# Second cross attention: row sums from ScalarE into spare PSUM columns, another order of VectorE's step, one transpose for the ones matmuls

## The chip, the cores and the metric

The kernel runs on one core of a Trainium2 chip. The metric is the device time of one execution in microseconds (us). The engines are TensorE (PE, with its weight loads as PEld), VectorE (DVE), ScalarE (ACT), GpSimd (POOL) and SyncE (SP), which issues DMAs. Each has its own queue and they meet at semaphores.

## The reference

The input x has 32 blocks of 128 tokens with 128 features; each block has a context of 77 rows with 128 features. Four parts follow each other, each added to x: a cross attention with 16 heads of 64, a mixture of 8 experts (two per token), a second cross attention, and two layers of local attention with a gated feed-forward. The change is in the second cross attention:

```
x = x + L1_xattn(layernorm(x), ctx, ctx, mask)
q, k, v = layernorm(x) @ w_q.T, ctx @ w_k.T, ctx @ w_v.T     (16 heads of 8)
s = q k^T / sqrt(8), masked where mask == 0                  (128 x 77 per head)
out = softmax(s) @ v, heads joined, @ w_o.T
```

## The kernel before

The second cross attention is a software pipeline over the 32 blocks. In step i each engine runs its `body`, which works on several blocks at once: `it.b(n)` is block i - n. `c_tensor`, `c_scalar`, `c_vector` and `c_pool` hold the bodies. The pipeline is unrolled by hand; within a step the order of each engine's queue is the order of the code. Steps 0 to 3 interleave with the end of the experts, and steps 35 to 38 with steps 0 to 2 of the first layer (`c_into_d`). After steps 11, 15, 19 and 23 ScalarE and VectorE each split one layer weight into a high and a low part (L1290, L1296).

The stages of one block b, by lag:

- lag 0 and 1: GpSimd gathers the two expert answers of each token; VectorE adds them to X with their weights (L1446) and takes the row statistics (L1450 to L1455); GpSimd takes the root (L1043).
- lag 2: VectorE normalizes (L751), TensorE turns the block (L1379), VectorE evicts it (L1485).
- lag 3: TensorE projects queries, keys and values (L1351 to L1353) into PSUM slot 0; ScalarE evicts the high parts (L1407 to L1411); VectorE makes the low parts and the two key blocks, one for each part (L1459 to L1468). Semaphore `c_sp` counts these.
- lag 4: TensorE makes the scores in two halves of 8 heads, slot 2 and slot 3, two banks each: first a matmul that lays the mask (L1335), then three passes (L1340). In each bank 4 x 77 = 308 of 512 columns are used. VectorE takes the maxima of a half (`largest`, L1427), and ScalarE writes the 8 exponentials of that half to `c_p` (`exponentials`, L741).
- lag 5: TensorE turns the 8 probability blocks of a half (L1321) into slot 1, ScalarE evicts them to `c_pT` (L1397), once per half; the second half's transposes wait until the first half is evicted. Then TensorE multiplies by the values (L1367) and, with the same moving data, by blocks of ones (L1372): this gives the row sums, laid out as the output is. VectorE takes their reciprocal, 128x128 (L1480), and multiplies (L1482).
- lag 6: TensorE applies w_o (L1383), VectorE adds to X (L1487) and takes the statistics (L1491, L1036, L1038); GpSimd takes the root, which the first layer uses.

Orders of one step before. TensorE: transposes of half 0 (lag 5), scores of half 0 (lag 4), transposes of half 1, scores of half 1, projections, P times V and ones, transpose of the normalized block, w_o. ScalarE: `c_pT` of half 0, `c_pT` of half 1, exponentials of half 0, evictions of the projections, exponentials of half 1. VectorE: layernorm, maximum of half 0, maximum of half 1, expert answers and statistics, low parts and key blocks, reciprocal and product, eviction of the turned block, addition to X and statistics. The scores of a half wait for that half's exponentials of the step before (`ac_expa`, `ac_expb`), since they overwrite the same bank.

Of the kernel before, what the change touches and what calls it, by code (L numbers as in the profile page):

```python
# [12 lines left out]
ALU = mybir.AluOpType  # L13
# [3 lines left out]
NB = 32  # L17
# [95 lines left out]
def program(nc, out, x_in, ctx_in, mask_in, wq0_in, wkv0_in, wo0_in, nrm0_in, wg_in, w1e_in, w3e_in, w2e_in,  # L113
            l1_in, wqkv_in, qks_in, wol_in, lng_in, w1l_in, b1l_in, w2l_in,
            ident_in, band_in, rot_in, keyi_in, head_in):
    with ExitStack() as ctx:
# [34 lines left out]
        onesz = at("onesz", [128, 4, 4, DH1])  # L151
# [134 lines left out]
        c_["p"] = at("c_p", [128, 2, 16, SK])  # L286
        c_["rcT"] = at("c_rcT", [128, 128])
# [109 lines left out]
        def split_dve(e):  # L397
# [6 lines left out]
            e.memset(onesz[:], 0.0).then_inc(S("const"), 1)  # L404
# [10 lines left out]
            e.wait_ge(S("const"), 4)  # L415
            for j in range(4):
                e.memset(onesz[:, j, j, :], 1.0).then_inc(S("c_const"), 1)
# [56 lines left out]
        def a_tensor(e):  # L474

            e.wait_ge(S("split"), 2)
            e.wait_ge(S("const"), 4)
# [259 lines left out]
        def exponentials(e, t, slot, half, nbank, nk, done, scale=None, head=lambda h: h):  # L737
# [559 lines left out]

        def c_tensor(e):
            t = c_

            def body(it):
                if it.static and it.i == 2:
                    e.wait_ge(S("b_xl"), LAST + 1)
                    e.wait_ge(S("c_const"), 5)
# [5 lines left out]
                for half, slot in ((0, 2), (1, 3)):  # L1310
# [34 lines left out]
                if b is not None:  # L1345
# [3 lines left out]
                    e.wait_ge(S("ac_ch"), count(b, base=NB))  # L1349
                    c = t["c"][:, it.m(3, 4), :]  # L1350
# [11 lines left out]
                if b is not None:  # L1362
# [7 lines left out]
                    for j in range(4):  # L1370
# [16 lines left out]
        def c_scalar(e):  # L1387
            t = c_

            def body(it):  # L1390
                if it.static and it.i == 3:
                    e.wait_ge(S("c_const"), 5)
                b = it.b(5)
                if b is not None:
                    for half in range(2):
                        e.wait_ge(S(("ac_PTa", "ac_PTb")[half]), count(b, base=NB))
# [3 lines left out]
                if b is not None:  # L1400
                    p = {"p": t["p"][:, it.m(4, 2), :, :], "nm": t["nm"]}
                    e.wait_ge(S("ac_mxa"), count(b, base=NB))
                    exponentials(e, p, 2, 0, 4, SK, S("ac_expa"))
# [10 lines left out]
                if b is not None:  # L1414
                    e.wait_ge(S("ac_mxb"), count(b, base=NB))
                    exponentials(e, p, 3, 1, 4, SK, S("ac_expb"))
            return body

        def c_vector(e):
# [9 lines left out]

            def body(it):  # L1430
                b = it.b(2)
# [3 lines left out]
                b = it.b(4)  # L1435
                if b is not None:
                    largest(b, 0, 2)
                    largest(b, 1, 3)
# [18 lines left out]
                if b is not None:  # L1457
# [11 lines left out]
                                    blocks, ALU.mult).then_inc(S("c_sp"), 1)  # L1469
                b3, b4, b0 = it.b(5), it.b(6), it.b(2)  # L1470
# [15 lines left out]
                if b4 is not None:  # L1486
# [680 lines left out]
```

## Time and profile before

| | us |
|---|---|
| median of 3 runs | 1606.81 |
| lowest and highest | 1605.17, 1607.92 |
| the profiled execution | 1606.48 |
| its span, first to last instruction | 1604.3 |

Shares of the span in which each engine is busy: TensorE 91%, VectorE 76%, ScalarE 70%, GpSimd 57%. The mean granted TensorE clock is 0.98 of full speed. The second cross attention's pipeline runs from about 597 to 861 us of the span, overlapped at both ends with its neighbours. In the rows, a start in us from the span's first instruction comes first, then the length; starts are what an engine's queue is measured by, since the end of one instruction overlaps the start of the next.

### The profile page before, as it was taken

What the parts mean: (1) busy time and instruction counts of PE and PEld (TensorE: products, weight loads), DVE (VectorE), ACT (ScalarE), POOL (GpSimd) and SP (SyncE); (2) the same over time, 40 slices, a digit from 0 to 9 for tenths busy, and PEclk for the clock granted to TensorE, in tenths of its full rate; (3) what the DMA queues carried; (4) which work ended last, traced back from release to release, by engine and by line L of the source; (5) the groups of instructions that cost most, each with busy time, mean ns of one, the idle gap of its engine ahead of it and who ended that gap; (6) DMA issues with size and microseconds to landing.
All of it is one profiled execution on the core that took longest, in us unless ns stands there. A gap on an engine that the chain in (4) does not pass through costs nothing.

```text
span 1604.3 us, 38573 instructions
## 1 busy us (share of the span) xinstructions
PE 1465.3 (91%) x12380; PEld 1212.1 (76%) x12443; DVE 1226.6 (76%) x3032; ACT 1121.2 (70%) x2666; POOL 910.4 (57%) x789
## 2 busy tenths in 40 slices
PE   4899999999888998999996999999898899999988
PEld 3677777777767876777775888888776788888766
DVE  6888888888856557888886788888566778787765
ACT  4888888877754556888784787878633787878732
POOL 4667778777842104555424777777402777777500
PEclk8999999999999997999997999999999999999999
DMA  9800000000012322100000000000000000000000
GB/s 381 330 1 8 11 10 10 10 11 18 11 50 80 85 72 67 35 19 18 17 11 9 14 14 16 14 16 14 10 10 5 7 14 16 13 16 14 10 25 33
DMA packets 75553, 61.29 MB, mean 38 GB/s; under 512 B 40256, under 2 KB 61120, under 8 KB 74688
## 3 DMA queue, kind: packets, MB, share of 16 engines
q1 hardware_dynamic: 71360, 51.69, 10.0%
q0 software_dynamic: 4096, 8.40, 1.8%
q8 instruction: 50, 0.82, 0.2%
q14 instruction: 47, 0.39, 0.1%
HBM read 21.30 MB, written 30.41 MB: 32 GB/s over the span
## 4 chain that ended last, share of the span: by engine, by line
PE 50%; DVE 32%; ACT 8%; issue 6%; POOL 3%; DMA 1%; DVEq 1%; SPq 0%; POOLq 0%; ACTq 0%
PE slot L1642 6%; PE slot L459 5%; PE slot L461 4%; PE slot L460 4%; PE slot L1625 4%; PE slot L1586 4%; PE slot L1660 3%; PE slot L1595 3%; ACT a_p L741 3%; DVE a_sum L859 3%; PE slot L1895 2%; POOL a_rq L1104 2%; DVE c_nm L1427 2%; DVE a_ssq L969 2%; PE slot L1636 2%
## 5 line engine op out<-in xcount | busy, mean ns | idle before, releaser
L1043 POOL TENSOR_TENSOR rs<-mv,nhalf 128x1 f32 (+1 forms) x160 | 98.9, 618 | 232.3 <-DVE mv L1038 165.0
L1811 POOL TENSOR_TENSOR d_A<-d_A,d_B 128x1024 f32<-128x1024 f32 x64 | 150.7, 2355 | 132.2 <-DVE d_B L1749 132.2
L1815 POOL TENSOR_TENSOR d_r<-d_vv,nhalf 128x16 f32<-128x16 f32 x64 | 186.4, 2913 | 46.9 <-DVE d_vv L1771 46.4
L741 ACT ACTIVATE d_p<-slot,d_nm,d_r 128x128 f32<-128x128 f32 x512 | 185.6, 468 | 27.1 <-DVE d_nm L1762 27.1
L741 ACT ACTIVATE a_p<-slot,a_nm,a_rq 128x77 f32<-128x77 f32 x512 | 163.7, 432 | 55.2 <-DVE a_nm L766 55.2
L741 ACT ACTIVATE c_p<-slot,c_nm 128x77 f32<-128x77 f32 x512 | 117.4, 361 | 8.9 <-DVE c_nm L1427 8.8
L1642 PE MATMUL slot<-d_v,d_pT 128*128 128x65 f32 x1024 | 121.8, 272 | 1.7 <-ACT d_pT L1679 1.7
L1642 PEld LDWEIGHTS slot<-d_v,d_pT 128*128 128x128 f32 x1024 | 119.4, 192 | 2.4 <-ACT d_pT L1679 2.1
L748 POOL TENSOR_TENSOR a_p<-a_p,a_rc 128x616 f32<-128x616 f32 x64 | 80.1, 1251 | 70.1 <-DVE a_rc L861 69.6
L1730 DVE TENSOR_TENSOR d_A<-slot,T 128x1024 f32<-128x1024 f32 x64 | 78.3, 1224 | 44.6 <-PE slot L1586 44.6
L1758 DVE TENSOR_REDUCE slot<-slot 128x8 f32<-128x1024 f32 x64 | 78.9, 1233 | 27.8 <-PE slot L1625 25.2
L1104 POOL TENSOR_TENSOR a_rq<-a_vvq,nhalf 128x16 f32<-128x16 f32 x32 | 95.0, 2968 | 1.8 <-DVE a_vvq L976 1.8
L1397 ACT ACTIVATE c_pT<-slot 77x1024 f32<-77x1024 f32 x64 | 66.8, 1044 | 40.2 <-PE slot L1321 40.1
L1690 ACT ACTIVATE d_oT<-slot 128x512 f32<-128x512 f32 x64 | 38.2, 597 | 78.7 <-PE slot L1636 78.7
L624 PE MATMUL slot<-a_kb,a_qT 128*128 128x154 f32 x512 | 81.1, 301 | 10.8 <-DVE a_pT L902 10.2
L1923 ACT ACTIVATE f_gl<-slot,b1l 128x512 f32<-128x512 f32 (+1 forms) x48 | 32.8, 684 | 77.5 <-PE slot L461 77.5
L1525 POOL DMA_INDIRECT c_yg<-answers,c_gi x64 | 64.1, 1002 | 36.7 <-POOL c_gi L1521 26.4
L1059 POOL DMA_INDIRECT routed<-r_xn,r_ps x64 | 64.8, 1013 | 34.3 <-issue 21.8
L624 PEld LDWEIGHTS slot<-a_kb,a_qT 128*128 128x128 f32 x512 | 69.7, 190 | 19.2 <-DVE a_pT L902 17.4
L1625 PEld LDWEIGHTS slot<-d_qT 64*128 64x128 f32 x1024 | 62.1, 187 | 27.1 <-issue 27.1
L1586 PE MATMUL slot<-ident,d_A 128*128 128x128 f32 x512 | 71.8, 285 | 11.6 <-ACT d_p L741 11.6
L1749 DVE TENSOR_TENSOR d_B<-slot,T 128x512 f32<-128x512 f32 x128 | 81.9, 682 | 0.0
(288 smaller groups left out, 4531.8 us busy)
## 6 DMA issues: line engine op xcount, KB each, us to landing
routed<-zero SPq DMA_DIRECT2D x2, 9216.0 KB, 49.3
b_x<-routed SPq DMA_DIRECT2D x80, 64.0 KB, 1.8
answers<-b_y SPq DMA_DIRECT2D x40, 128.0 KB, 1.9
X<-in_x SPq DMA_DIRECT2D x2, 1024.0 KB, 7.4
d_zx<-Z SPq DMA_DIRECT2D x64, 32.0 KB
H<-Z SPq DMA_DIRECT2D x64, 32.0 KB
out<-f_o SPq DMA_DIRECT2D x8, 256.0 KB, 2.0
d_zx<-Z SPq DMA_DIRECT2D x64, 31.8 KB
```

The costliest lines, as they stand in the source:

```text
L459: e.matmul(o, ws[1], xs[0], start=True, stop=False)
L624: mm = e.matmul(R[slot][:, k // 2, 2 * SK * (k % 2):2 * SK * (k % 2) + 2 * SK], a["qT"][:, c, :], a["kb"][:, it.m(2, 2), c // 2, :], start ...
L741: i = e.activation(t["p"][:, h, :], R[slot][:, k // nbank, nk * (k % nbank):nk * (k % nbank) + nk], ACT.Exp, bias=t["nm"][:, h:h + 1], sca ...
L748: return e.tensor_tensor(p, p, t["rc"][:, h].unsqueeze(2).to_broadcast([128, h.stop - h.start, nk]), ALU.mult)
L1043: return e.tensor_tensor(rs[:, bass.ds(b, 1)], mv[:, bass.ds(b, 1), 1:2].rearrange("p a b -> p (a b)"), nhalf[:, 0:1], ALU.pow)
L1104: e.tensor_tensor(a["rq"][:, it.m(1, 2), :], a["vvq"][:], nhalf[:, 0:16], ALU.pow).then_inc(S("a_rq"), 1)
L1586: mm = e.transpose(R[2][:, c // 4, 128 * (c % 4):128 * (c % 4) + 128], t["A"][:, it.m(4, 2), 128 * c:128 * c + 128], ident[:])
L1625: mm = e.matmul(R[2][:, h % 2, 128 * (h // 2):128 * (h // 2) + 128], t["qT"][o:o + DL, h // 2, :], t["qT"][o:o + DL, 4 + h // 2, :], start ...
L1642: mm = e.matmul(R[3][:, h // 4, 65 * (h % 4):65 * (h % 4) + 65], t["pT"][:, 4 * (h % 2) + h // 2, :], t["v1"][:, it.m(5, 4), h, :], start= ...
L1749: i = e.tensor_tensor(Bt[:, :, :, 32 * h:32 * h + 32], qk[:, :, :, 32 - 32 * h:64 - 32 * h], T2[:, l, :, 32 * h:32 * h + 32].unsqueeze(2). ...
L1811: e.tensor_tensor(t["A"][:, p, :], t["A"][:, p, :], t["B"][:, p, :], ALU.add).then_inc(S("d_key"), 1)
L1815: e.tensor_tensor(t["r"][:, it.m(2, 4), :], t["vv"][:, p, :], nhalf[:, 0:16], ALU.pow).then_inc(S("d_key"), 1)
```

## The change

- ScalarE's exponentials of this stage also put out their row sum (`accum_out`), one column per head, into columns 308 to 315 of the second bank of the score slots (`totals`).
- VectorE takes the reciprocal of those 8 columns per half (`shares`): half 0 at the end of the key blocks in the same step as the exponentials (lag 4, semaphore `c_rca`), half 1 in the next step (lag 5, `c_rcb`), and copies the 16 values to `c_rx`, each spread over the 8 columns of its head.
- TensorE turns `c_rx` in one transpose into the PSUM columns where the ones matmuls wrote; these and their constant `onesz` are gone. VectorE's 128x128 reciprocal becomes a copy.
- The scores of a half wait for `c_rca` or `c_rcb` in place of `ac_expa` or `ac_expb`.
- Four transposes of the identity, whose result nobody reads, stand ahead of the projections.
- ScalarE's order: `c_pT` of half 0, exponentials of half 0, `c_pT` of half 1, evictions, exponentials of half 1; and one Exp of two elements in step 3.
- VectorE's order: maximum of half 0, addition to X and statistics (now lag 7, GpSimd's root with it), reciprocal of half 1 and the spread copy, maximum of half 1, layernorm, expert answers and statistics, low parts and key blocks, reciprocal of half 0, copy and product, eviction of the turned block.

```diff
+        totals = [R[2 + half][:, 1, 4 * SK:4 * SK + 8] for half in range(2)]
...
 def exponentials(...):
-                                 bias=t["nm"][:, h:h + 1], scale=1.0 if scale is None else scale[:, head(h):head(h) + 1])
+                                 bias=t["nm"][:, h:h + 1], scale=1.0 if scale is None else scale[:, head(h):head(h) + 1],
+                                 accum_out=None if total is None else total[:, k:k + 1])
...
 def c_tensor(e):
-                        if half == 0:
-                            if it.seen(5):
-                                e.wait_ge(S("ac_expa"), it.upto(5, NB))
-                        else:
-                            if it.seen(5):
-                                e.wait_ge(S("ac_expb"), it.upto(5, NB))
+                        if it.seen(5):
+                            e.wait_ge(S(("c_rca", "c_rcb")[half]), it.upto(5))
...
+                    for k in range(4):
+                        e.transpose(R[0][:, 0, 384:512], ident[:], ident[:])
...
-                    for j in range(4):
-                        for g in range(4):
-                            mm = e.matmul(R[0][32 * g:32 * g + 32, 1, 384:512],
-                                          onesz[0:SK, j, :, :].rearrange("p a b -> p (a b)"), t["pT"][0:SK, 4 * g + j, :],
-                                          start=(j == 0), stop=(j == 3))
-                    mm.then_inc(S("ac_PV"), 1)
+                    e.wait_ge(S("c_rx"), count(b))
+                    e.transpose(R[0][:, 1, 384:512], t["rx"][:].rearrange("p a b -> p (a b)"), ident[:]).then_inc(S("ac_PV"), 1)
...
 def c_scalar(e):
+                if it.static and it.i == 3:
+                    e.activation(warm[:], eps[:, 0, :], ACT.Exp)
+                b4, b5 = it.b(4), it.b(5)
+                for half in range(2):
+                    if b5 is not None:
+                        e.wait_ge(S(("ac_PTa", "ac_PTb")[half]), count(b5, base=NB))
                         e.activation(t["pT"][0:SK, 8 * half:8 * half + 8, :].rearrange("p (a c) t -> p a (c t)", a=2),
                                      R[1][0:SK, :, :], ACT.Copy).then_inc(S(("ac_pTa", "ac_pTb")[half]), 1)
+                    if half == 0 and b4 is not None:
+                        p = {"p": t["p"][:, it.m(4, 2), :, :], "nm": t["nm"]}
+                        e.wait_ge(S("ac_mxa"), count(b4, base=NB))
+                        exponentials(e, p, 2, 0, 4, SK, S("ac_expa"), total=totals[0])
...
 def c_vector(e):
+            def shares(b, m, half):
+                e.wait_ge(S(("ac_expa", "ac_expb")[half]), count(b, base=NB))
+                e.reciprocal(t["rc"][:, m, 8 * half:8 * half + 8], totals[half]).then_inc(S(("c_rca", "c_rcb")[half]), 1)
+
             def body(it):
+                b = it.b(4)
+                if b is not None:
+                    largest(b, 0, 2)
+                b = it.b(7)
+                if b is not None:
+                    e.wait_ge(S("ac_wo"), count(b, base=NB))
+                    e.tensor_tensor(rows(X, b), rows(X, b), R[0][:, 1:2, 256:384], ALU.add).then_inc(S("ac_add"), 1)
+                    e.wait_ge(S("ac_add"), count(b, base=NB))
+                    apart(e)
+                    e.bn_stats(st[:, 0, :], rows(X, b)).then_inc(S("ac_bn"), 1)
+                    stats_tail(e, b, S("ac_bn"), S("ac_ag"), S("ac_ve"), base=NB)
+                b = it.b(5)
+                if b is not None:
+                    m = it.m(5, 2)
+                    shares(b, m, 1)
+                    e.wait_ge(S("c_rca"), count(b))
+                    e.wait_ge(S("c_rcb"), count(b))
+                    e.tensor_copy(t["rx"][:], t["rc"][:, m, :].unsqueeze(2).to_broadcast([128, 16, DH1])).then_inc(S("c_rx"), 1)
+                b = it.b(4)
+                if b is not None:
+                    largest(b, 1, 3)
                 b = it.b(2)
                 if b is not None:
                     e.wait_ge(S("c_rs"), count(b))
                     layernorm(e, X, t["xn"], b, it.m(2, 2)).then_inc(S("ac_xn"), 1)
-                b = it.b(4)
-                if b is not None:
-                    largest(b, 0, 2)
-                    largest(b, 1, 3)
...
+                b = it.b(4)
+                if b is not None:
+                    shares(b, it.m(4, 2), 0)
...
-                    e.reciprocal(t["rcT"][:], R[0][:, 1, 384:512]).then_inc(S("c_rcT"), 1)
+                    e.tensor_copy(t["rcT"][:], R[0][:, 1, 384:512]).then_inc(S("c_rcT"), 1)
```

## Rows read from the trace of the kernel before

**Rows 1.** The page: busy us (share of the span) xinstructions, VectorE.

```profile
PE 1465.3 (91%) x12380; PEld 1212.1 (76%) x12443; DVE 1226.6 (76%) x3032; ACT 1121.2 (70%) x2666; POOL 910.4 (57%) x789
```

**Rows 2.** Chain of waits, 700 to 760 us: shares by line.

```profile
by line: DVE c_nm L1427 19.0%; issue 15.7%; DVE c_rcT L1480 11.7%; DVE X L1446 8.4%; DVE c_kbl L1468 6.3%; DVE st L1491 4.6%; DVE st L1450 4.1%; DVE c_oT L1482 3.9%; DVE ac_xn L751 3.7%; DVE c_qTl L1459 3.4%; DVE X L1487 3.1%; DVE c_xT L148
```

**Rows 3.** VectorE in order: start us, us, line, out<-in xcount.

```profile
635.66 1.50 DVE L1427 TENSOR_REDUCE c_nm<-slot 128x8 f32<-128x616 f32 x2
...
710.52 1.50 DVE L1427 TENSOR_REDUCE c_nm<-slot 128x8 f32<-128x616 f32 x2
711.94 0.73 DVE L1446 SCALAR_TENSOR_TENSOR X<-c_yg,r_w,X 128x128 f32<-128x128 f32 x2
712.82 0.29 DVE L1450 BATCH_NORM_STATS2 st<-X 128x6 f32<-128x128 f32 x1
...
714.38 0.47 DVE L1468 TENSOR_TENSOR c_kbl<-c_kl,head 128x308 fp32r<-128x308 f32 x1
714.76 0.95 DVE L1480 RECIPROCAL c_rcT<-slot 128x128 f32<-128x128 f32 x1
715.75 0.29 DVE L1482 TENSOR_TENSOR c_oT<-slot,c_rcT 128x128 f32<-128x128 f32 x1
...
716.16 0.28 DVE L1487 TENSOR_TENSOR X<-X,slot 128x128 f32<-128x128 f32 x1
...
717.33 0.34 DVE L751 TENSOR_SCALAR ac_xn<-X,mv,rs 128x128 f32<-128x128 f32 x1
717.58 1.50 DVE L1427 TENSOR_REDUCE c_nm<-slot 128x8 f32<-128x616 f32 x2
...
842.84 0.80 DVE L1427 TENSOR_REDUCE c_nm<-slot 128x8 f32<-128x616 f32 x1
```

**Rows 4.** Windows: busy us of PE, PEld, DVE, ACT, POOL; clock, DMA share, GB/s.

```profile
710.52:717.58 7.06, 6.77 (x107) 5.35 (x105) 6.32 (x20) 5.62 (x22) 3.63 (x6) 1.00 0.07 19
814.41:821.87 7.46, 7.04 (x109) 5.62 (x107) 6.35 (x20) 5.88 (x22) 3.58 (x7) 1.00 0.08 20
```

**Rows 5.** Timeline: two score groups, and a maximum that waited.

```profile
627.89 0.43 PE L1335 MATMUL slot<-maskb,identb 128*128 128x308 bf16 x2
...
628.98 0.80 DVE L1427 TENSOR_REDUCE c_nm<-slot 128x8 f32<-128x616 f32 x1 [0.58 <-PE slot L1340]
...
714.91 0.44 PE L1335 MATMUL slot<-maskb,identb 128*128 128x308 bf16 x2
```

**Rows 6.** Groups, DVE: count | busy us, mean ns | idle before, releaser.

```profile
L1777 DVE RECIPROCAL d_rc<-slot 128x8 f32<-128x8 f32 x64 | 12.9, 202 | 12.9 <-PE slot L1642 12.9
```

**Rows 7.** Timeline of the same step: ScalarE, then TensorE.

```profile
711.35 1.83 ACT L741 ACTIVATE c_p<-slot,c_nm 128x77 f32<-128x77 f32 x8 [0.25 <-DVE c_nm L1427]
713.02 0.33 ACT L1407 ACTIVATE c_qTh<-slot 128x128 fp32r<-128x128 f32 x1
...
713.45 1.85 ACT L741 ACTIVATE c_p<-slot,c_nm 128x77 f32<-128x77 f32 x8
715.10 1.11 ACT L1397 ACTIVATE c_pT<-slot 77x1024 f32<-77x1024 f32 x1
717.40 1.02 ACT L1397 ACTIVATE c_pT<-slot 77x1024 f32<-77x1024 f32 x1 [1.19 <-PE slot L1321]
...
712.53 1.06 PE L1372 MATMUL slot<-c_pT,onesz 77*32 77x128 f32 x32
...
713.91 1.04 PE L1321 MATMUL slot<-ident,c_p 128*77 128x128 f32 x8
```

**Rows 8.** Groups by line and form: ScalarE's shortest instruction.

```profile
L1706 ACT ACTIVATE warm<-eps 128x2 f32<-128x2 f32 x2 | 0.4, 203 | 0.0
```

**Rows 9.** Window as in rows 4; TensorE beside a weight split.

```profile
610.00:620.00 10.00, 9.64 (x46) 7.07 (x45) 5.24 (x15) 5.00 (x20) 5.06 (x7) 0.50 0.20 69
...
701.45 1.10 PE L1321 MATMUL slot<-ident,c_p 128*77 128x128 f32 x8 [1.45 <-ACT c_pT L1397]
```

More of the change, by code:

```diff
@@ L150, in program @@
         maskb = at("maskb", [128, 4, SK], BF16)
-        onesz = at("onesz", [128, 4, 4, DH1])
         nhalf = at("nhalf", [128, 32])
@@ L286, in program @@
         c_["p"] = at("c_p", [128, 2, 16, SK])
+        c_["rc"] = at("c_rc", [128, 2, 16])
+        c_["rx"] = at("c_rx", [128, 16, DH1])
         c_["rcT"] = at("c_rcT", [128, 128])
@@ L403, in split_dve @@
             e.wait_ge(S("eps"), 3)
-            e.memset(onesz[:], 0.0).then_inc(S("const"), 1)
             e.memset(a["kb"][:], 0.0).then_inc(S("const"), 1)
@@ L476, in a_tensor @@
             e.wait_ge(S("split"), 2)
-            e.wait_ge(S("const"), 4)
+            e.wait_ge(S("const"), 3)
             e.wait_ge(S("counted"), 9)
@@ L735, in a_scalar, with exponentials @@
             return tiles
-        def exponentials(e, t, slot, half, nbank, nk, done, scale=None, head=lambda h: h):
+        def exponentials(e, t, slot, half, nbank, nk, done, scale=None, head=lambda h: h, total=None):
             for k in range(2 * nbank):
@@ L1303, in body @@
                     e.wait_ge(S("b_xl"), LAST + 1)
-                    e.wait_ge(S("c_const"), 5)
+                    e.wait_ge(S("c_const"), 1)
                 if it.static and it.i == 4:
@@ L1369, in body @@
                                           start=(j == 0), stop=(j == 3))
-                    for j in range(4):
-                        for g in range(4):
-                            mm = e.matmul(R[0][32 * g:32 * g + 32, 1, 384:512],
-                                          onesz[0:SK, j, :, :].rearrange("p a b -> p (a b)"), t["pT"][0:SK, 4 * g + j, :],
-                                          start=(j == 0), stop=(j == 3))
-                    mm.then_inc(S("ac_PV"), 1)
+                    e.wait_ge(S("c_rx"), count(b))
+                    e.transpose(R[0][:, 1, 384:512], t["rx"][:].rearrange("p a b -> p (a b)"), ident[:]).then_inc(S("ac_PV"), 1)
                 b = it.b(2)
@@ L1391, in body @@
                 if it.static and it.i == 3:
-                    e.wait_ge(S("c_const"), 5)
-                b = it.b(5)
-                if b is not None:
-                    for half in range(2):
-                        e.wait_ge(S(("ac_PTa", "ac_PTb")[half]), count(b, base=NB))
+                    e.wait_ge(S("c_const"), 1)
+                if it.static and it.i == 3:
[4 more added lines that the diff above has]
+                        e.wait_ge(S(("ac_PTa", "ac_PTb")[half]), count(b5, base=NB))
                         e.activation(t["pT"][0:SK, 8 * half:8 * half + 8, :].rearrange("p (a c) t -> p a (c t)", a=2),
                                      R[1][0:SK, :, :], ACT.Copy).then_inc(S(("ac_pTa", "ac_pTb")[half]), 1)
-                b = it.b(4)
[L1400 to L1403, printed above, removed]
+                    if half == 0 and b4 is not None:
+                        p = {"p": t["p"][:, it.m(4, 2), :, :], "nm": t["nm"]}
+                        e.wait_ge(S("ac_mxa"), count(b4, base=NB))
+                        exponentials(e, p, 2, 0, 4, SK, S("ac_expa"), total=totals[0])
                 b = it.b(3)
@@ L1415, in body @@
                     e.wait_ge(S("ac_mxb"), count(b, base=NB))
-                    exponentials(e, p, 3, 1, 4, SK, S("ac_expb"))
+                    exponentials(e, p, 3, 1, 4, SK, S("ac_expb"), total=totals[1])
             return body
@@ L1434, in body @@
                     layernorm(e, X, t["xn"], b, it.m(2, 2)).then_inc(S("ac_xn"), 1)
-                b = it.b(4)
-                if b is not None:
-                    largest(b, 0, 2)
-                    largest(b, 1, 3)
                 b = it.b(1)
@@ L1485, in body @@
                     e.tensor_copy(t["xT"][:, it.m(2, 2), :], R[0][:, 1, 128:256]).then_inc(S("ac_xh"), 1)
-                if b4 is not None:
-                    e.tensor_tensor(rows(X, b4), rows(X, b4), R[0][:, 1:2, 256:384], ALU.add).then_inc(S("ac_add"), 1)
-                if b4 is not None:
-                    e.wait_ge(S("ac_add"), count(b4, base=NB))
-                    apart(e)
-                    e.bn_stats(st[:, 0, :], rows(X, b4)).then_inc(S("ac_bn"), 1)
-                    stats_tail(e, b4, S("ac_bn"), S("ac_ag"), S("ac_ve"), base=NB)
                 if it.static and it.i in (5, 6):
@@ L1537, in body @@
                     e.tensor_copy(c_["c"][:, m:m + 1, :], rows(ctx_sb, b)).then_inc(S("ac_ch"), 1)
-                b = it.b(6)
+                b = it.b(7)
                 if b is not None:
```

2 lines of the change are left out of this document (removed).

## The prediction

> **What bounds the stage now.** I read four views in this order. The page first: VectorE is busy 76% of the whole span [rows 1], but that averages stages with different limits, so it says nothing of this one. Second, the chain of waits over 60 us in the middle of the second cross attention: its shares are nearly all VectorE lines, the maxima with 19.0% and the reciprocal with 11.7% on top, and no TensorE or ScalarE line among the leading ones [rows 2]. Third, the stretch of one step: the step takes 7.06 us (first maximum to first maximum), in which TensorE is busy 6.77, VectorE 6.32 and ScalarE 5.62 [rows 4]. Fourth, the order of VectorE's instructions in that step [rows 3]: one starts as soon as the other allows, except for some 0.15 us after the statistics of a row. So VectorE's queue is the bound and the step is as long as that queue. TensorE and ScalarE have little to spare, though: ScalarE waits 1.19 us in each step, for the second half's transposes [rows 7].
>
> From the first maximum of step 7 to that of step 35 there are 28 steps in 207.18 us [rows 3], 7.40 each. Of the surplus over 7.06, the four splits of layer weights between steps make the greater part, and some of the last steps take 7.42 to 7.46 [rows 4].
>
> **The change, part by part.** I sum VectorE's start-to-start intervals, since ends overlap.
>
> Taken from VectorE's queue: the reciprocal of 128x128 in PSUM. Reciprocal to product is 0.99 us [rows 3]. A copy in its place should keep one at about 0.33 (a 128x128 product there takes 0.29, with a short wait behind it): 0.66 saved.
>
> Added to it: two reciprocals of 128x8 from PSUM. The layer stage has this operation, with the same shape, at 202 ns [rows 6]. Bounds: 0.08 to 0.23 us each, by what it holds up behind it; I take 0.20. Also the copy that spreads 16 values over 128 columns: 0.20, bounded by 0 and the 0.35 of the layernorm row of like size [rows 3]. It is covered below, because VectorE then waits anyway. Counted as a queue alone, VectorE would come out at 7.06 - 0.66 + 0.60 = 7.00: no change.
>
> But two waits are new, and they lie across the queue. Both are in TensorE's score groups, which now may not start until VectorE has read the row sums in the bank that they write.
>
> (1) The second half's scores of step i wait for c_rcb of the same step i. VectorE makes that reciprocal behind the first maximum, the residual addition and the row statistics. Then it has only the 0.20 us copy to do before it needs the second maximum, for which these scores must be done. In the kernel before they waited for the exponentials of the last step, long over, so the two maxima stand back to back in 1.42 us [rows 3].
>
> (2) The first half's scores of step i+1 wait for c_rca, which VectorE makes in step i behind the key blocks. Between it and the next first maximum stand only the copy, the product and the turned block, some 0.8 us.
>
> What such a turn costs the trace shows: a score group starts at 627.89 and VectorE, which waited for it 0.58 us, starts its maximum at 628.98, 1.09 later; from the end of the last key block (714.38 + 0.47) to the start of the group behind it there are 0.06 [rows 5]. I take 1.14 from the end of a small reciprocal to the start of the maximum. In the trace this turn is nearly always hidden beside other VectorE work; in the new order only 0.20 and some 0.8 us stand beside the two.
>
> So the new step is a closed chain that goes twice through TensorE. From the first maximum to the second: the maximum 0.71 (half of 1.42), addition through statistics 1.17 (716.16 to 717.33), reciprocal 0.20, turn 1.14: 3.22 us. From the second maximum to the next first: maximum 0.71, layernorm 0.25 (717.33 to 717.58), the two weighted additions 0.88 (711.94 to 712.82), statistics and the split of queries and keys 1.56 (712.82 to 714.38), last key block 0.38 (714.38 to 714.76), reciprocal 0.20, turn 1.14: 5.12 us [rows 3, 5, 6]. Together 8.34 us against 7.06: 1.28 us more, of which about 0.9 is VectorE idle behind the row-sum reciprocal and 0.3 at the end of the step. With 0.08 for a reciprocal and 1.09 for a turn the step is 8.0; with 0.23 and 1.2 it is 8.5.
>
> ScalarE. It now turns pT's first half, takes the first eight exponentials where it used to wait 1.19 us, then the second half. Its work is 1.10 + 1.67 + 1.02 + 0.43 + 1.65 = 5.87 us per step [rows 7], with 2.47 us of room in a step of 8.34. Into that go 16 outputs of a sum. No row shows that operation. Below: nothing, if it hides in the exponential's pipeline. Above: each exponential runs to its end and a least instruction behind it: 0.37 us (1.83 less seven intervals) instead of the 0.209 at which they follow each other (1.67 / 8), and 0.203 for two elements [rows 7, 8]: 0.36 us. Nearest is the 0.14 us that each of three short evictions takes in the queue (0.43 / 3) [rows 7], less their elements; I take 0.1, 1.6 us per step, and it fits. Up to 0.154 us each it costs nothing; beyond that ScalarE is the bound at 5.87 us plus 16 times the price.
>
> TensorE. The 32 ones matmuls took about 0.8 us in the step (1.06 less the last one's 0.27 of latency); one transpose takes 0.11 and the four fillers ahead of the projections 0.44, at eight in 1.04 less the same latency [rows 7]. That is 0.25 saved, on an engine that now idles about 1 us at c_rcb. The fillers lie ahead of the projections, whose evictions VectorE needs before it splits the queries: the scores end at 3.2 us after the first maximum, the fillers at 3.7, the projections (six matmuls, bounded by the eight transposes' 1.04) by 4.7, the evictions (0.43 and 0.3 of latency) by 5.4. VectorE comes for them at 3.22 + 0.71 + 0.25 + 0.88 and then 0.8 of statistics (1.17 less the addition and its wait), 5.9. The cover is 0.5 us.
>
> Moves that cost nothing by themselves: the addition to X now comes a step later; TensorE waits for it only ahead of P times V, at about 4.4 us, and it is done at 1.0; GpSimd's root moves with it and feeds only the layer stage. SP issues nothing in these steps. The early Exp loads a table that was loaded in a wait anyhow; the memsets at the start lie beside the first load of X. The splits between steps: ScalarE's part comes later behind its second exponentials, VectorE's copy in its old idle; these about cancel (within 2 us in all). At the end of the stage a shorter TensorE path (no ones, no long reciprocal) stands against later second exponentials; I take 0, within 3.
>
> **Sum.** 28 steps times 1.28 = 35.8 us. The profiled execution took 1606.48 us with a span of 1604.3; so 1642.3, and as it lies 0.3 below the median of 1606.81, about 1642.
>
> **Rivals.**
>
> (A) The queue alone counts, and it comes out faster. If the turn were hidden, the step would be 7.00, or 6.88 with reciprocals cheaper by 0.12 in all; 28 times 0.18 is 5 us, with 2 to 3 at the end: 1599. For it speak the queue-bound rows [rows 2, 3]. It needs 1.14 us of VectorE work between c_rcb and the second maximum; there are 0.20. It decides from there, and I see no way round it. The Trainium skill (Perfetto Trace Analysis, Identifying the Most-Contended Engine) says to improve the engine with the highest occupancy first. By that rule alone, taking 0.66 us off VectorE would count in full and this rival would hold; the wait of 0.58 us on scores in [rows 5] shows that order can outweigh occupancy.
>
> (B) The sum outputs make ScalarE the bound. At 0.25 us each the step is 5.87 + 4.0 = 9.87, 28 times 2.81 = 79: 1685. At the full 0.36 it would be 1734. For it: a dependent read behind each exponential; against: how tightly short instructions follow each other.
>
> (C) TensorE's clock. It was granted 0.50 (1.2 of 2.4 GHz) at the head of this stage [rows 9]. With the change it idles about 1.2 us in every step of 8.3. Against: a gap of 1.45 us beside a weight split left it at full speed [rows 9]. If half of the steps ran at half clock, each with two turns up to twice as long (2 x 1.09), that is 14 times up to 2.2: 30 more, up to 1672. The Trainium skill (TensorE: Matmul & The Clock Gate, HAM oscillation) warns that repeated small idles of TensorE can make its clock swing.
>
> **Chances.** Main case 0.60, its own range 1630 to 1652 (steps of 8.0 to 8.5, ends within 5). B 0.16, C 0.12, A 0.07. Left 0.05: the gain and the loss nearly meet, 1603 to 1625. The range 1620 to 1686 leaves out A, most of the rest, and the upper part of B. A change within 0.2% (3.2 us) can't be told from none. Faster 0.06, same 0.03, slower 0.91.
>
> **What would show it.** Right: VectorE idle 0.8 to 1.0 us before the second maximum, released by TensorE's scores, and TensorE idle about 1 us before the second half's mask matmul, released by the reciprocal; a step of about 8.3; ScalarE's wait for transposes gone. Wrong: two maxima still back to back (A); ScalarE without idle and with more than 0.15 us per sum (B); score groups longer than 1.1 us at a granted clock below 1 (C).

## The result, and the profile after

| | before | after |
|---|---|---|
| median us | 1605.17 (5 runs) | 1647.33 (5 runs) |
| lowest and highest | 1601.08, 1607.92 | 1645.76, 1651.71 |
| profiled execution, its span | 1606.48, 1604.3 | 1651.71, 1649.9 |
| clean step of the stage | 7.06 | 8.45 |

The ratio is 1.0271, 95% interval 1.0253 to 1.0288: slower by 42 us. The prediction was 1642, slower. The profiled execution of after is the slowest of its five, 4.4 us over the median.

The page of after, the line that answers to [rows 1]. VectorE's share fell from 76% to 74% and the kernel became slower.

```profile
PE 1474.3 (89%) x11516; PEld 1212.4 (73%) x11579; DVE 1222.4 (74%) x3123; ACT 1154.0 (70%) x3179; POOL 911.9 (55%) x789
```

The chain of waits, 700 to 760 us, by line, as in [rows 2]. TensorE's score and mask matmuls (L1336, L1331) now stand in it with 19.0%; before, no TensorE line led.

```profile
by line: DVE c_nm L1422 14.6%; issue 14.0%; PE slot L1336 11.8%; PE slot L1331 7.2%; DVE X L1462 5.3%; DVE c_kbl L1484 3.9%; ACT c_p L738 3.5%; PE slot L1365 3.1%; DVE st L1439 3.0%; PE slot L1347 2.7%; DVE st L1466 2.5%; DVE c_rc L1427 2.3
```

VectorE in order, as in [rows 3]: start, length, and in brackets the idle time ahead and who ended it.

```profile
633.43 0.80 DVE L1422 TENSOR_REDUCE c_nm<-slot 128x8 f32<-128x616 f32 x1 [0.53 <-PE slot L1336]
...
735.51 0.80 DVE L1422 TENSOR_REDUCE c_nm<-slot 128x8 f32<-128x616 f32 x1 [0.55 <-PE slot L1336]
...
737.39 0.20 DVE L1427 RECIPROCAL c_rc<-slot 128x8 f32<-128x8 f32 x1
737.70 0.23 DVE L1447 COPY c_rx<-c_rc 128x128 f32<-128x128 f32 x1
738.82 0.80 DVE L1422 TENSOR_REDUCE c_nm<-slot 128x8 f32<-128x616 f32 x1 [0.90 <-PE slot L1336]
...
742.52 0.20 DVE L1427 RECIPROCAL c_rc<-slot 128x8 f32<-128x8 f32 x1
742.64 0.24 DVE L1499 COPY c_rcT<-slot 128x128 f32<-128x128 f32 x1
742.91 0.29 DVE L1501 TENSOR_TENSOR c_oT<-slot,c_rcT 128x128 f32<-128x128 f32 x1
...
743.96 0.80 DVE L1422 TENSOR_REDUCE c_nm<-slot 128x8 f32<-128x616 f32 x1 [0.56 <-PE slot L1336]
...
887.94 0.80 DVE L1422 TENSOR_REDUCE c_nm<-slot 128x8 f32<-128x616 f32 x1 [0.60 <-PE slot L1336]
```

Each step has two waits on scores, 0.90 and 0.56 us. TensorE, in the same step, shows what held the scores: the small reciprocals.

```profile
737.73 0.42 PE L1331 MATMUL slot<-maskb,identb 128*128 128x308 bf16 x2 [1.23 <-DVE c_rc L1427]
...
742.87 0.42 PE L1331 MATMUL slot<-maskb,identb 128*128 128x308 bf16 x2 [0.41 <-DVE c_rc L1427]
```

Windows, as in [rows 4]: the clean step, and a step in which TensorE's granted clock was mostly 0.50, its lower level (1.2 of 2.4 GHz).

```profile
735.51:743.96 8.45, 6.82 (x79) 5.27 (x80) 6.16 (x23) 6.88 (x37) 3.71 (x6) 1.00 0.06 16
822.11:834.71 12.60, 11.20 (x79) 8.70 (x80) 6.38 (x22) 6.96 (x37) 5.71 (x8) 0.60 0.06 16
```

In the clean step all three main engines are idle for over 1.5 us: it is a chain through two engines, not the queue of one.

ScalarE, as in [rows 7]: each sum is an instruction of its own, and the exponentials follow each other at 0.26 us where they followed at 0.209.

```profile
736.35 0.33 ACT L738 ACTIVATE c_p<-slot,c_nm 128x77 f32<-128x77 f32 x1 [1.09 <-DVE c_nm L1422]
736.57 0.17 ACT L738 ACTIVATION_READ_ACCUMULATOR c_p<-slot,c_nm 128x1 f32 x1
736.62 0.33 ACT L738 ACTIVATE c_p<-slot,c_nm 128x77 f32<-128x77 f32 x1
```

**Where the 45.6 us of the two spans went.** From the first maximum of step 7 to that of step 35: 207.18 us before [rows 3], 254.51 after (887.94 - 633.43), 47.3 more. Ahead of it after is 2.2 shorter, behind it 0.5 longer. Of the 47.3, the clean steps make 28 x (8.45 - 7.06) = 38.9. The rest is surplus over clean steps, 9.5 us before and 17.9 after, in three parts. Four steps at a lower clock add 12.7 (11.04, 11.29, 12.60 and 11.60 us long; the first two follow a step with a weight split). The splits cost 1.4 less. What is left is 3.8 before and 0.9 after: the late steps 24 to 31 carry 3.6 before, and after 2.2 (8.76 to 8.97 each) without the two slow ones among them, while the last two steps are 1.3 shorter than a clean one after and 0.3 before. Why the late steps are longer in both kernels no run shows.

A second pair of traces, c1 (before) and c2 (after), has stages of 207.30 and 255.65 us with clean steps of 7.07 and 8.44, and in c2 the same four steps at a lower clock. There the stretch ahead of the stage is 1.2 us longer after and that behind it 3.7, so the -2.2 and +0.5 above lie within what single executions scatter by and can't be put down to the change.

### The profile page after: what moved, and what is told of

The parts are those of the page before. It is cut to its first block, busy times and chain, and to the rows that moved or that the text cites. A ratio compares the mean times of both kernels' runs of the same rounds, so it can differ in the third digit from the quotient of the medians.

```text
span 1649.9 us, 37493 instructions
## 1 busy us (share of the span) xinstructions
PE 1474.3 (89%) x11516; PEld 1212.4 (73%) x11579; DVE 1222.4 (74%) x3123; ACT 1154.0 (70%) x3179; POOL 911.9 (55%) x789
## 4 chain that ended last, share of the span: by engine, by line
PE 54%; DVE 27%; ACT 8%; issue 6%; POOL 3%; DMA 1%; DVEq 1%; SPq 0%; POOLq 0%; ACTq 0%
PE slot L1654 6%; PE slot L456 5%; PE slot L458 4%; PE slot L457 4%; PE slot L1637 4%; PE slot L1598 4%; PE slot L1672 3%; PE slot L1607 3%; ACT a_p L738 3%; DVE a_sum L857 3%; PE slot L1336 2%; PE slot L1907 2%; POOL a_rq L1102 2%; DVE a_ssq L967 2%; PE slot L1648 2%
## 5 line engine op out<-in xcount | busy, mean ns | idle before, releaser
L738 ACT ACTIVATE c_p<-slot,c_nm 128x77 f32<-128x77 f32 x512 | 143.6, 375 | 37.1 <-DVE c_nm L1422 37.0
L738 ACT ACTIVATION_READ_ACCUMULATOR c_p<-slot,c_nm 128x1 f32 x512 | 114.6, 226 | 0.0
L1422 DVE TENSOR_REDUCE c_nm<-slot 128x8 f32<-128x616 f32 x64 | 51.2, 799 | 52.5 <-PE slot L1336 52.5
L1683 ACT ACTIVATE d_qT<-slot 128x1024 f32<-128x1024 f32 x64 | 65.7, 1027 | 23.4 <-PE slot L1598 23.4
```

## The experiments

There were three sets, each on another chip and with fresh runs of the kernel before. "Stage" is the time from the first maximum of step 7 to that of step 35 in the profiled execution, "clean step" the interval of first maxima at full clock away from weight splits, and "low" the number of the 28 steps whose mean granted clock is below 0.95.

| kernel | set | median (range) us | stage | clean step | low |
|---|---|---|---|---|---|
| before | 1 | 1640.21 (1637.69 to 1647.06) | | | |
| e1 | 1 | 1642.03 (1637.96 to 1646.04) | 231.2 | 7.88 | 2 |
| e2 | 1 | 1633.84 (1632.55 to 1639.06) | 224.6 | 7.67 | 2 |
| e3 | 1 | 1668.21 (1658.45 to 1676.06) | 250.9 | 8.44 | 6 |
| e4 | 1 | 1645.61 (1644.70 to 1651.85) | 240.2 | 8.37 | 0 |
| before (stage and step: c1) | 2 | 1603.98 (1600.71 to 1608.16) | 207.3 | 7.07 | 0 |
| after (c2) | 2 | 1648.10 (1645.61 to 1655.70) | 255.7 | 8.44 | 4 |
| e5 | 2 | 1670.96 (1665.89 to 1675.58) | 263.1 | 8.42 | 9 |
| e6 | 2 | 1663.93 (1661.49 to 1666.10) | 261.0 | 7.89 | 21 |
| before | 3 | 1604.72 (1603.10 to 1606.95) | | | |
| n1 | 3 | 1644.65 (1643.23 to 1654.34) | 246.1 | 8.45 | 2 |
| n2 | 3 | 1608.63 (1604.57 to 1611.74) | 209.7 | 7.26 | 0 |
| e7 | 3 | 1610.76 (1606.80 to 1618.65) | 214.5 | 7.40 | 0 |
| e2 again (r2) | 3 | 1625.30 (1622.80 to 1626.92) | 225.8 | 7.67 | 2 |

**Set 1 was not normal.** The kernel before took 1640 us there and 1604 in both others, with mean granted clocks of 0.975 to 0.983, as in the others (0.977 to 0.985), so TensorE's clock is not the reason. Its own profile was not taken in that set, so the 36 us can't be placed, and whether it was the chip or something else stays open. The four profiled kernels lost some 10 us ahead of the stage: they reach step 7 at 643.6 to 645.7 us, where all the others reach it at 633.2 to 639.0. By VectorE's starts, 7 to 10 us of it go in one stretch, 446 to 488 us, among the experts, and up to there they keep within 1 us of the first trace of after. Against that set's kernel before, the ratios would be 1.0001 (e1), 0.9968 (e2), 1.0178 (e3) and 1.0036 (e4). I don't use them; stages and steps are compared. That these held is shown for one kernel: e2 has a clean step of 7.67 in both sets and stages of 224.6 and 225.8. e1, e3 and e4 ran in set 1 only.

Two controls stood in set 2. The kernel before against itself, meant to trace the 1640 us, which did not come back:

> The kernel before, unchanged, for its trace on this chip, where its runs have a median of 1640.21 us against 1606.81 on the first chip. Theory P (the chip): a step of the second cross attention is longer here, above 7.06 us, by the lower clock or slower gathers, and the ratio of changed to before is smaller here. If the step is still 7.06 the surplus lies outside the stage, and both kernels should have it.

It read 1603.24, ratio 1.0001 (0.9987 to 1.0016). The kernel after:

> The changed kernel, unchanged, on this chip, as the base for the experiments. From the experiment with the eight more transposes (1645.6) and the one without the fillers (1668.2) I expect 1648 to 1660 us and a ratio to before of 1.005 to 1.012; if the surplus of before is outside the stage, 1.027 as on the first chip.

Ratio 1.0263 (1.0233 to 1.0292): the result repeats.

**e1: sums in SBUF, no wait on reciprocals.**

```diff
+        c_["ts"] = at("c_ts", [128, 2, 16])
...
-                            e.wait_ge(S(("c_rca", "c_rcb")[half]), it.upto(5))
+                            e.wait_ge(S(("ac_expa", "ac_expb")[half]), it.upto(5, NB))
...
-                        exponentials(e, p, 2, 0, 4, SK, S("ac_expa"), total=totals[0])
+                        exponentials(e, p, 2, 0, 4, SK, S("ac_expa"), total=t["ts"][:, it.m(4, 2), 0:8])
```

> The changed kernel with one thing undone: the row sums go to a tile in SBUF with two buffers instead of the PSUM columns beside the scores, so the scores wait for the exponentials of the step before, as in the kernel before. VectorE's order, the fillers and the one transpose stay. Theory T (the two turns through TensorE): the 0.90 us and 0.55 us that VectorE waits in a step of 8.44 go, the step is about 7.0 us, the time 1603 to 1610 (ratio to before 0.998 to 1.003). Rival S (ScalarE's sum outputs and its new order): the step stays above 8 us and the time above 1635, since all 16 outputs are still there. Rival K (TensorE's clock alone): only the 13 us of the half-clock steps go, about 1634.

A miss. The wait ahead of the second maximum went, as the theory of the two turns says, but the step fell only to 7.88, not to about 7.0. VectorE, ScalarE and TensorE of e1 in one step:

```profile
740.46 0.80 DVE L1422 TENSOR_REDUCE c_nm<-slot 128x8 f32<-128x616 f32 x1 [0.94 <-PE slot L1336]
...
742.78 0.79 DVE L1422 TENSOR_REDUCE c_nm<-slot 128x8 f32<-128x616 f32 x1
...
748.34 0.80 DVE L1422 TENSOR_REDUCE c_nm<-slot 128x8 f32<-128x616 f32 x1 [0.94 <-PE slot L1336]
```

```profile
741.29 0.33 ACT L739 ACTIVATE c_p<-slot,c_nm 128x77 f32<-128x77 f32 x1 [0.67 <-DVE c_nm L1422]
...
743.71 1.03 ACT L1393 ACTIVATE c_pT<-slot 77x1024 f32<-77x1024 f32 x1
```

```profile
744.88 1.08 PE L1365 MATMUL slot<-c_pT,c_vz 77*32 77x128 f32 x32 [1.01 <-ACT c_pT L1393]
...
746.39 1.04 PE L1321 MATMUL slot<-ident,c_p 128*77 128x128 f32 x8
747.26 0.42 PE L1331 MATMUL slot<-maskb,identb 128*128 128x308 bf16 x2
```

The waits and releasers of these rows close a second chain, which I had not seen: maximum (740.46), eight exponentials (741.29 to 743.71, at 0.30 us each), eviction of the second half, P times V (744.88), the turned blocks and w_o, P transposed (746.39), scores (747.26), maximum (748.34): 7.88. The change made it, by putting the eight exponentials ahead of the second eviction; before, they stood behind both. It was hidden below the 8.45 of the first chain.

**n1 and n2: the same two kernels without the sum outputs.** The exponentials put out sums for the first block (n1) or the first two (n2) only; the rest is divided by old values.

```diff
-                        exponentials(e, p, 2, 0, 4, SK, S("ac_expa"), total=totals[0])
+                        exponentials(e, p, 2, 0, 4, SK, S("ac_expa"), total=None if not (it.static and it.i in (4,)) else totals[0])
...
```

> The kernel after, but the exponentials put out row sums only for the first block, so later blocks are divided by old sums; waits, reciprocals and order are unchanged. Turn theory (T): the step of 8.44 us is VectorE's path twice through TensorE, on which no sum output lies: it stays at 8.4 to 8.45, time 1643 to 1650; ScalarE only idles 0.8 us more. Rival (S), the sum outputs are on the path that sets the step: it falls by up to 16 x 0.05 = 0.8 us, to 7.65, time about 1625.

> As e1 (sums in SBUF, scores no longer wait for a reciprocal), but row sums only for the first two blocks. T with a second loop through ScalarE, in which the first half's eight exponentials lie (they follow at 0.30 in e1, 0.209 without the sum): e1's step of 7.88 falls by at least 8 x 0.09 = 0.72 to 7.0 to 7.15, VectorE's queue being the bound again, time 1603 to 1612. Rival, it is the order of ScalarE (the second half's probabilities turned behind the exponentials) and not the sum outputs that makes e1's step long: the step stays over 7.5, time over 1620.

VectorE of n1, then of n2:

```profile
735.43 0.80 DVE L1422 TENSOR_REDUCE c_nm<-slot 128x8 f32<-128x616 f32 x1 [0.56 <-PE slot L1336]
...
738.74 0.80 DVE L1422 TENSOR_REDUCE c_nm<-slot 128x8 f32<-128x616 f32 x1 [0.90 <-PE slot L1336]
...
743.88 0.80 DVE L1422 TENSOR_REDUCE c_nm<-slot 128x8 f32<-128x616 f32 x1 [0.55 <-PE slot L1336]
```

```profile
738.40 0.80 DVE L1422 TENSOR_REDUCE c_nm<-slot 128x8 f32<-128x616 f32 x1 [0.36 <-PE slot L1336]
...
740.73 0.79 DVE L1422 TENSOR_REDUCE c_nm<-slot 128x8 f32<-128x616 f32 x1
...
745.66 0.80 DVE L1422 TENSOR_REDUCE c_nm<-slot 128x8 f32<-128x616 f32 x1 [0.36 <-PE slot L1336]
```

This is the plainest evidence of the study. n1 keeps the waits, drops all but 16 of ScalarE's 512 sum outputs, and its step does not move (8.45, waits 0.90 and 0.56). Its stage is 8.4 us shorter than after's all the same, with two steps at a lower clock instead of four; as the clean step stayed, this is no price of the sums on the chain. n2 drops the waits too, and the step is 7.26, the time 1608.63: ratio to before 1.0028 (1.0018 to 1.0037). So the price of the two turns is at least 8.45 - 7.26 = 1.19 us a step with the sums away. And e1 less n2, 7.88 - 7.26 = 0.62, is what sum outputs into SBUF cost once the turns are gone. n2 also prices what else the change brought, ScalarE's new order with the rest: 7.26 against 7.06. n2's step is 0.1 over the most I expected. Its 0.36 us of wait on scores ahead of the first maximum says that the second chain is still in it; that chain with eight exponentials at 0.209 instead of 0.30 would be 7.88 - 0.73 = 7.15.

**e5: the kernel before with sum outputs to an unused SBUF tile.**

```diff
+                                 accum_out=None if total is None else total[:, k:k + 1])
...
-                    exponentials(e, p, 2, 0, 4, SK, S("ac_expa"))
+                    exponentials(e, p, 2, 0, 4, SK, S("ac_expa"), total=t["ts"][:, it.m(4, 2), 0:8])
```

> The kernel before with sum outputs alone: ScalarE's 512 exponentials of the stage also write their row sums, to an unused tile in SBUF; the ones matmuls, the long reciprocal and every order and wait stay. In the experiment with the sums in SBUF the exponentials follow each other every 0.30 us instead of 0.21, so ScalarE's 5.87 us become 7.3, and with its wait of 1.19 us for the transposes 8.5 a step. Theory S2 (ScalarE's place in the loop counts): 28 times 1.2 to 1.5, so 33 to 42 us slower than before. If the sum outputs were free, as I forecast up to 0.154 us each: within 3 us of before.

It is 67 us slower, 1.0408 (1.0369 to 1.0446), more than either reading; the clean step, 8.42, is what theory S2 forecast. ScalarE in e5, in order; the bracket is the wait of [rows 7], unchanged:

```profile
826.84 1.02 ACT L1399 ACTIVATE c_pT<-slot 77x1024 f32<-77x1024 f32 x1 [1.19 <-PE slot L1323]
827.76 0.31 ACT L742 ACTIVATE c_p<-slot,c_nm 128x77 f32<-128x77 f32 x1
827.97 0.20 ACT L742 ACTIVATION_READ_ACCUMULATOR c_p<-slot,c_nm 128x1 f32 x1
828.06 0.32 ACT L742 ACTIVATE c_p<-slot,c_nm 128x77 f32<-128x77 f32 x1
...
835.26 1.02 ACT L1399 ACTIVATE c_pT<-slot 77x1024 f32<-77x1024 f32 x1 [1.19 <-PE slot L1323]
```

In that order ScalarE's step is its work and the 1.19, which it can't give up; in the kernel before, all that is left over is the 0.25 ahead of the exponentials [rows 7]. Sixteen exponentials at 0.30 instead of 0.209 add 1.46, less 0.25 of slack: the 8.42 measured, within 0.2. The other 18 us of the stage (263.1 - 207.2 - 28 x 1.36) go with a lower clock: nine of its 28 steps had a mean granted clock of 0.50 to 0.94, where the kernel before had 1.00 in all of them.

**e2 and its repeat r2: the second half's reciprocal and the spread copy first in VectorE's step.**

```diff
             def body(it):
+                b = it.b(5)
+                if b is not None:
+                    m = it.m(5, 2)
+                    shares(b, m, 1)
...
                 b = it.b(4)
                 if b is not None:
                     largest(b, 0, 2)
```

> The changed kernel with one placement moved: the second half's reciprocal and the spread copy stand ahead of VectorE's first maximum instead of behind the residual addition and its statistics. The sums stay in PSUM and all waits stay. Theory T: the second half's scores find c_rcb done, the turn of 1.43 us from the start of that reciprocal to the second maximum leaves the chain, and the reciprocal and copy (0.5 us) fill the wait ahead of the first maximum; the step is about 7.05 us, the time 1605 to 1613. Rival S: unchanged, above 1635. Rival K: if only the clock matters, about 1634.

> e2 again, word for word, on another chip beside fresh runs of the kernel before. If the 1640 us of the kernel before in the first set was a property of that set and not of the program, the kernel before reads 1600 to 1608 here and this one 1630 to 1637: ratio 1.016 to 1.020, in line with the steps (7.67 us against 7.06).

VectorE of e2:

```profile
737.65 0.80 DVE L1422 TENSOR_REDUCE c_nm<-slot 128x8 f32<-128x616 f32 x1 [0.43 <-PE slot L1336]
...
745.32 0.80 DVE L1422 TENSOR_REDUCE c_nm<-slot 128x8 f32<-128x616 f32 x1 [0.42 <-PE slot L1336]
...
747.51 0.80 DVE L1422 TENSOR_REDUCE c_nm<-slot 128x8 f32<-128x616 f32 x1 [0.25 <-PE slot L1336]
```

The long turn is covered (0.25 us of wait is left of 0.90), but the step is 7.67, not the 7.05 that I expected: a miss. By its length it is the second chain again, with exponentials at 0.26 (7.88 less eight times 0.04 is 7.56); e7 puts that to the test. The repeat gives 1.0130 (1.0113 to 1.0147), a better time than I expected of it (1630 to 1637).

**e7: e2 with P times V last in TensorE's step**, so that the two transposes and w_o leave the second chain.

```diff
                 b = it.b(5)
                 if b is not None:
-                    e.wait_ge(S("ac_pTb"), count(b, base=NB))
-                    for j in range(4):
...
                     e.wait_ge(S("c_rx"), count(b))
...
                         .then_inc(S("ac_wo"), 1)
+                b = it.b(5)
+                if b is not None:
+                    e.wait_ge(S("ac_pTb"), count(b, base=NB))
+                    for j in range(4):
...
+                    mm.then_inc(S("ac_PV"), 1)
```

> As e2 (reciprocal and spread copy first in VectorE's step, sums in PSUM), and in TensorE's step the turned sums, the turned normalized block and w_o stand ahead of P times V. If e2's 7.67 us is the loop P transposed, evicted, eight exponentials, second eviction, P times V, w_o, P transposed, the three transposes and w_o (some 0.45 us) leave it: 7.2 to 7.3 us a step, 1617 to 1624. Rival, e2 is bound by the two short VectorE waits on scores (0.42 and 0.26) and the order of TensorE's tail is beside the point: 7.6 to 7.7, 1630 to 1636.

```profile
742.72 0.80 DVE L1425 TENSOR_REDUCE c_nm<-slot 128x8 f32<-128x616 f32 x1
...
745.25 0.80 DVE L1425 TENSOR_REDUCE c_nm<-slot 128x8 f32<-128x616 f32 x1 [0.57 <-PE slot L1336]
```

The steps alternate between 7.66 and 7.13, 7.40 in the mean; 1610.76, ratio 1.0043 (1.0026 to 1.0059). Taking some 0.45 us out of the second chain shortened the mean step by 0.27, where the rival had it unchanged: TensorE's tail does lie on the path of e2. I had forecast 7.2 to 7.3, and why the steps alternate no run shows. The time is better than the 1617 to 1624 expected; r2, the base of that forecast, was itself better than expected, and of the 11.3 us that e7's stage is shorter than r2's some 4 are r2's two steps at a lower clock, of which e7 has none. This is the best version that computes the whole reference with the new sums, 37 us better than the change, and still 6 us behind the kernel before. Nothing that I ran beats that.

**e3: no fillers. e4: eight more fillers, in TensorE's wait for the second half's reciprocal.**

```diff
-                    for k in range(4):
-                        e.transpose(R[0][:, 0, 384:512], ident[:], ident[:])
```

And e4:

```diff
+                        if half == 1:
+                            for k in range(8):
+                                e.transpose(R[0][:, 0, 384:512], ident[:], ident[:])
                         if it.seen(5):
                             e.wait_ge(S(("c_rca", "c_rcb")[half]), it.upto(5))
```

> The changed kernel without the four transposes of the identity ahead of the projections. Theory T with the clock as a second term: the undisturbed step stays at 8.44 us (they lie in cover), but TensorE is less busy, so more of the stage runs at the lower clock: 3 to 30 us slower than the changed kernel. Rival F (the fillers delay the evictions and so the chain): the step gets shorter by up to 0.45 us, 12 us faster than the changed kernel. If the clock does not care, the same within 3 us.

> The changed kernel with eight more transposes of the identity on TensorE just ahead of its wait for c_rcb, about 0.9 us of work in a wait of about 1.2 us. Theory T with the clock as a second term: the step stays at 8.44 us, the half-clock stretches in the middle of the stage (37 us of them in the trace after) go, and with them about 13 us: some 1635. If the half-clock steps were not caused by TensorE's idle time, they stay and the time is that of the changed kernel, 1647. If the fillers delay the scores, more than 1650.

e4's stage, as a window:

```profile
633.00:890.00 257.00, 229.40 (x2575) 182.41 (x2574) 188.07 (x651) 211.00 (x1122) 103.08 (x164) 1.00 0.07 17
```

The clock is 1.00 throughout, no step is a slow one, and the stage is 14.3 us shorter than after's 254.5: 12.1 less surplus and 2.2 from steps of 8.37. The time, 1645.61, is not the 1635 that I expected but that of the changed kernel, which was the reading against the clock; the trace speaks for it all the same, since its span is after's 1649.9 less 14.3 in the stage and 2.8 behind it, plus 10.2 of set 1's loss ahead. It rests on one traced execution in set 1; other executions of e4, up to 1651.85 us, had mean clocks down to 0.976.

e3's clean step stays at 8.44, so the four fillers delay nothing. Its profiled execution, the fastest of the four (1658.45), has a stage like after's (250.9) but six steps at a lower clock instead of four. The slower executions have no trace, but their mean granted clocks fall as their times grow: 0.967 at 1658.45 us, 0.958 at 1666.64, 0.953 at 1669.78 and 0.945 at 1676.06, where c2 had 0.969 to 0.977. That fits the forecast of a lower clock without fillers; where in the kernel it was lower no trace shows.

**e6: e1 with one reciprocal of 16 columns and the spread copy first, no fillers.**

```diff
-                    for k in range(4):
-                        e.transpose(R[0][:, 0, 384:512], ident[:], ident[:])
...
+                    e.reciprocal(t["rc"][:, m, :], t["ts"][:, m, :]).then_inc(S("c_rcb"), 1)
```

> The changed kernel with the sums in two SBUF buffers, one reciprocal of 128x16 and the spread copy ahead of the first maximum, the scores waiting for the exponentials again, and without the four fillers. VectorE's queue falls by 0.3 us a step against the experiment with the reciprocal first, but the loop through ScalarE (maximum, eight exponentials with sum at 0.30, second eviction, P times V, transposes, scores, maximum) stays at 7.9 us. Theory L (that loop is the second bound): a step of 7.9 and a time as in the experiment with the sums in SBUF, 1642, plus what the clock takes without fillers. If VectorE's queue were the bound: 6.8 a step, 25 us faster than that.

1663.93, ratio 1.0367. The steps at full clock take 7.89, as theory L forecast: VectorE's shorter queue gains nothing over e1's 7.88, so VectorE's queue is not what the second chain waits for. The rest of the loss is clock: 0.79 over the stage.

```profile
633.00:890.00 257.00, 218.34 (x2023) 172.82 (x2014) 175.50 (x574) 203.49 (x1013) 96.39 (x155) 0.79 0.06 16
...
771.13 1.99 PE L1321 MATMUL slot<-ident,c_p 128*77 128x128 f32 x8
...
779.57 1.10 PE L1321 MATMUL slot<-ident,c_p 128*77 128x128 f32 x8
```

The same eight transposes take 1.99 or 1.10 us, in steps 8.4 us apart. A chain that waits on TensorE pays this on each turn. e6 differs from e1 (0.96 over the same window) by the fillers and by VectorE's order, and which of the two costs the clock wasn't separated.

## Why the prediction was right

By its own steps:

- **The queue alone** was to come out at 7.00 us. With the turns removed and no sum outputs it is 7.26 (n2), of which 0.36 is a wait on scores; the queue itself is then 6.9. The forecast is right within 0.1.
- **The two turns**: waits of 0.8 to 1.0 and about 0.3 us were forecast; they are 0.90 and 0.56. Right in place and releaser, and shown: n1 holds the step when only sums go, n2 loses 1.2 when the waits go. The second was mis-sized: from the start of a small reciprocal to the maximum are 1.43 (737.39 to 738.82) and 1.44 (742.52 to 743.96), where I had 0.20 + 1.14, and that reciprocal holds VectorE's queue for 0.12 (742.52 to 742.64), where I had 0.20. The turn itself, 1.23 and 1.24, was a little over the upper bound that I had named (1.2). The other signs came as named: TensorE idle 1.23 us before the second half's mask matmul, released by the reciprocal, and ScalarE's wait of 1.19 us for the transposes gone.
- **The step**: 8.34 forecast, 8.45 measured, inside 8.0 to 8.5; its two parts 3.31 and 5.14, where I had 3.22 and 5.12. That term gives 38.9 instead of 35.8 us.
- **The small reciprocal**: 0.20, as the layer stage's [rows 6].
- **Sum outputs**: I took 0.1 us each, bounded by 0 and 0.36, and free up to 0.154. They cost 0.05 into PSUM and are free in this order (n1: same step). But the argument "ScalarE has 2.47 us of room" was too coarse: room counts along a chain, not per step. In e1, where the first chain is cut, the same sums lie on the path (0.62 us, e1 less n2), and by the length of its step in e2 too, for which no run without sums was made; had the change's turn been cheaper than I thought, the time would have stopped at this second chain (7.67 to 7.9 us a step), not at the 7.00 of rival A. This is the step that the prediction lacks.
- **Clock (rival C)** was right in part beside the main case: four slow steps of 28, 12.7 us or 3.2 each, where I had reckoned 14 at up to 2.2 each for the rival and none for the main case. In the traced execution of e4 work put into the wait holds the clock at 1.00. For the main case this term was put at nothing, and that was wrong.
- **Ends and splits**: taken as 0 within 3 and as cancelling within 2. Measured: 2.2 less ahead, 0.5 more behind, splits 1.4 less, late and last steps 2.9 less. Together they hide half of the clock's loss (6.0 of 12.7). The two ends are within scatter (+1.2 and +3.7 from c1 to c2), and the account is that of the slowest execution: 1651.71, 9 us over the 1642.3 forecast for it. That the median lies only 5 us from 1642 is therefore in part luck; that the step was right is not.

Rivals A and B are refuted: TensorE's releases before both maxima, and 0.05 us a sum with 1.09 us of ScalarE idle beside it. By the Trainium skill's rule on the engine with the highest occupancy (Perfetto Trace Analysis, Identifying the Most-Contended Engine) A would have held. The page does not take TensorE's matmul time for that comparison but its weight loads, beside the FLOPs that it does; by weight loads the step before has VectorE highest (6.32 us, ScalarE 5.62, weight loads 5.35 [rows 4]), though TensorE's matmuls alone were busy for 6.77. VectorE's queue did set that step, but relieving it this way lengthened the step.

What stays open: the 1640 us of the kernel before in set 1; e1, e3 and e4 in a set where it reads 1604; why e7's steps alternate; how much of e6's loss is the fillers' absence; and why single steps of after, and always the same four in its two traces, fell to the lower clock.

## What to carry to other kernels

Before work is taken off a bound queue, list what each new semaphore makes a closed chain of, and walk that chain once round; a producer and its consumer's consumer close together in one queue cost the whole trip through the other engine (here 1.23 and 1.24 us, against 0.2 and some 0.8 us of work between them). Walk the next chain as well, since it is what the first one hides: moving eight exponentials ahead of an eviction was free here only because the step was already 8.45 us. If a wait can't be avoided, move its producer ahead, to where other work covers the trip (e2), or take the state out of the bank that is waited for (e1), before anything else. Here neither was enough: e1 and e2 shortened the step, and both still took longer steps than the kernel before.

## What the runs showed of the hardware

- An exponential with a sum output is two instructions in the trace. A 128x77 exponential then follows the last at 0.26 us with the sum in PSUM and 0.30 in SBUF, against 0.209 without. Why the destination in SBUF is the dearer one no run here shows.
- TensorE fell to its lower clock (0.50) in single steps. TensorE's idle time in a clean step and the number of steps at a lower clock among 28: before 0.23 us and none; e4, with eight transposes in the wait, 0.68 and none; n2 0.54 and none; e7 0.49 and none; e2 1.04 and two; e1 1.28 and two; n1 1.64 and two; after 1.63 and four; e3, without fillers, 2.0 and six; e6 1.8 and 21. The idle time alone does not order them (n1 beside after, e6 beside e3).
- The same program read 2% longer in one set of runs, on another chip, than in two others (1640 against 1604 us) at the same mean clock, while a variant of it moved by far less (e2 by 8.5 us). The clean step of e2 was the same in both sets (7.67).
